# In the first chunk, the high and low parts of a piece are made one unit earlier

## The reference

```
xn  = layernorm(x)
q   = xn @ wq.T                      # 16 heads of 128 (no position) + 64 (rotary)
kv  = xn @ wkv_a.T                   # latent of 128 + one rotary key of 64
kv_cache = rmsnorm(latent) * kv_norm_w
q_lat  = q_nope @ wkv_b[:, :128]     # per head, to the latent width
scores = (q_lat @ kv_cache.T + q_pe @ k_pe.T) * scale, causal
out    = softmax(scores) @ kv_cache @ wkv_b[:, 128:]   # per head
y = x + out @ wo.T + (xn @ ternary(w_ffn).T + b_ffn)
```

## Time and profile before

| | |
|---|---|
| median of 3 runs | 1833.46 us (1831.61 to 1834.55) |
| profiled execution | 1835.66 us, its span 1833.6 us |
| mean granted clock of PE | 0.974 of full speed |
| PE busy | 1715.1 us (94% of the span) |
| DVE, POOL, ACT busy | 1210.3, 1008.5, 848.9 us |
| first chunk, slots 0 to 15 | about 185 to 432 us of the span |

### The profile page before, as it was taken

The page is one execution under the profiler, slowest core; times in us unless marked ns, Lnnn a source line. Parts: engine busy times, 40 slices in busy tenths (PEclk is TensorE's granted clock), DMA queues, the critical chain, the costliest instruction groups (busy, mean ns, idle before and its releaser), DMA issues. The chain is left out here.

```text
span 1833.6 us, 28210 instructions
## 1 busy us (share of the span) xinstructions
PE 1715.1 (94%) x9326; PEld 1448.6 (79%) x9326; DVE 1210.3 (66%) x2801; ACT 848.9 (46%) x1358; POOL 1008.5 (55%) x635
## 2 busy tenths in 40 slices
PE   6998788888999999999999999999999999999996
PEld 5887677666777777778888888888888888888885
DVE  4765465665677667667777767767677666666763
ACT  4554344443444455345544554544544544554442
POOL 4674544443465555455565565565646555565654
PEclk9888899998999999999999999999999999999999
DMA  6995345464766666647555555566756565555553
GB/s 198 372 331 212 105 138 172 134 203 135 196 164 169 173 164 170 195 133 207 151 155 161 144 153 159 158 191 164 191 131 152 146 163 130 158 153 129 148 131 107
DMA packets 127680, 309.12 MB, mean 169 GB/s; under 512 B 29554, under 2 KB 42099, under 8 KB 126388
## 3 DMA queue, kind: packets, MB, share of 16 engines
q1 hardware_dynamic: 98784, 227.04, 44.0%
q10 hardware_dynamic: 28756, 80.35, 16.1%
HBM read 113.28 MB, written 34.60 MB: 81 GB/s over the span
## 5 line engine op out<-in xcount | busy, mean ns | idle before, releaser
L1416 POOL TENSOR_TENSOR pT<-pT,pT_h 128x1024 fp32r<-128x1024 f32 x320 | 688.8, 2181 | 419.8 <-ACT pT_h L1322 418.2
L1196 DVE TENSOR_SCALAR_CACHE_REDUCE probs<-p_score 128x512 f32<-128x512 f32 (+3 forms) x640 | 381.4, 602 | 370.4 <-PE p_score L1124 219.3
L1301 ACT ACTIVATE probs<-probs,neg_max 128x128 f32<-128x128 f32 (+15 forms) x256 | 307.6, 1202 | 438.0 <-DVE neg_max L1202 373.8
L1322 ACT ACTIVATE pT_h<-pT 128x1024 fp32r<-128x1024 f32 x320 | 291.3, 963 | 254.7 <-PE p_out L1144 173.6
L1218 DVE STREAM_TRANSPOSE turned<-probs 128x1024 f32<-128x1024 f32 (+7 forms) x384 | 341.6, 915 | 42.5 <-ACT probs L1301 38.0
L1144 PE MATMUL p_out<-pT_h,V_h 128*128 128x256 f32 (+3 forms) x1024 | 302.7, 296 | 26.6 <-POOL pT L1416 26.5
L1144 PE MATMUL p_out<-pT,V_h 128*128 128x256 f32 (+3 forms) x1024 | 304.2, 297 | 0.0
L1144 PE MATMUL p_out<-pT_h,V_l 128*128 128x256 f32 (+3 forms) x1024 | 303.7, 297 | 0.0
L1124 PE MATMUL p_score<-Kp,qp_h 128*128 128x512 f32 (+3 forms) x640 | 236.3, 369 | 15.3 <-POOL qp_l L1408 15.3
L1124 PE MATMUL p_score<-Kn_h,q_h 128*128 128x512 f32 (+3 forms) x640 | 241.6, 377 | 2.9 <-DVE q_l L1241 2.4
L1144 PEld LDWEIGHTS p_out<-pT_h,V_h 128*128 128x128 f32 x1024 | 196.8, 192 | 51.4 <-issue 34.8
(11 more groups left out here) (135 smaller groups left out, 2352.0 us busy)
## 6 DMA issues: line engine op xcount, KB each, us to landing
pT<-turned SPq DMA_DIRECT2D x384, 128.0 KB, 3.3
Wq<-wq_scr ACTq DMA_DIRECT2D x63, 512.0 KB, 4.7
Wv<-wv_scr SPq DMA_DIRECT2D x63, 512.0 KB, 4.0
pT<-turned SPq DMA_DIRECT2D x192, 112.0 KB, 3.8
pT<-turned SPq DMA_DIRECT2D x192, 96.0 KB, 2.5
pT<-turned ACTq DMA_DIRECT2D x128, 128.0 KB, 3.9
Wp<-wp_scr SPq DMA_DIRECT2D x31, 512.0 KB, 4.7
pT<-turned SPq DMA_DIRECT2D x192, 80.0 KB, 2.8
```

Source lines behind the costliest of these rows:

```text
L1196: dve.tensor_scalar(probs[row % ROW_RING][:, b * CW:b * CW + width], p_score[n % SCORE_RING][:, 0:width], SCALE, LOWEST, ALU.mult, ALU.max ...
L1301: act.activation(probs[row % ROW_RING][:, 0:width], probs[row % ROW_RING][:, 0:width], ACT.Exp, bias=neg_max[p][:, i:i + 1], scale=1.0, ac ...
L1322: act.activation(high.rearrange("p r t i q -> p r t (i q)"), low.bitcast(F32).rearrange("p r t i q -> p r t (i q)"), ACT.Copy).then_inc(p_ ...
L1416: pool.tensor_tensor(low.rearrange("p r t i q -> p r t (i q)"), low.bitcast(F32).rearrange("p r t i q -> p r t (i q)"), high.bitcast(F32). ...
```

## The change

One condition in `high_place`. For the first three groups of a piece whose next slot is in the first chunk (phase 0) the place is now unit 0 of slot s+2, where it was unit 1. Pieces 0 to 14 are concerned; piece 14's place is in slot 16, the first of the second chunk. All their groups have k below 3.

```diff
 def high_place(s, k):
 
     if k < HIGH_RING:
-        return (s + 1, units_of(s + 1) - 1) if phase(s + 1) == 1 else (s + 2, 0 if phase(s + 1) == 3 else 1)
+        return (s + 1, units_of(s + 1) - 1) if phase(s + 1) == 1 else (s + 2, 0 if phase(s + 1) in (0, 3) else 1)
     return s + 2, value_unit(s + 2, k - HIGH_RING)
```

## The result

The changed kernel took 1811.16 us in the median of 4 runs (1810.88 to 1812.61), the kernel before 1834.01 us in 4 runs beside it (1831.61 to 1838.35): ratio 0.9874, 95% interval 0.9855 to 0.9894. The forecast was 1815.3 us, with a range from 1810 to 1828. The gain is 22.9 us where 18.2 were forecast.

The account below looks back on a forecast made before the run. PE, busy 94% of the span, was taken as the bound. Terms 17.0 + 0.6 - 0.7 - 1.1 + 2.4 = 18.2 us gave 1815.3 us; own range 1811 to 1821, with rival 1 1810 to 1828.

Parts of the forecast that it names:

- What started the high groups: In odd slots, ACT's issue of the exchange DMAs, not landing data; start at 322.2 instead of 325.37 us in slot 9.
- POOL's order: In odd slots POOL starts the low groups only after the rotary addition, though the first high part came about a microsecond earlier.
- Odd slots: Slots 3 to 13: POOL wait of 1.49 us goes, plus 1.6 of low clock in five slots; 17.0 us gained.
- Slot 2: The first slot concerned loses its wait of 0.6 us.
- The slack: In odd slots PE could start at about 325.9 us and is ready at 328.31: 2.4 us of slack.
- The new wait for L1408: Even slots: PE waits about 1.45 us for the low rotary query at the fourth score product, covering the `Wv` wait.
- Even slots 4 to 12: 7.3 us of new waits, less 4.6 for `Wv` and 2.0 for POOL: net loss 0.7 us, bounds 0 to 3.
- Slots 14 and 15: ACT comes later to the load of `xT` in slot 14, needed in slot 15: loss 1.1 us, bounds 0 and 2.2.
- Slot 16: Groups start 2.4 us earlier, cutting PE's 2.63 us wait for POOL: gain 2.4 us, bounds 0 and 2.63.
- half of the clock's share not won: Slow end of the forecast's own range, 1821 us: half the gain from avoiding the low clock fails.
- Rival 1: Clock falls behind the new wait in even slots, six times 1.6 us: 1825 us; chance 0.24.
- Rivals 2 and 3: Odd slots: late landing keeps PE's wait, 1832 us, chance 0.10; or blocks ACT's exponential and exchange, 1843.5 us, chance 0.08.

Follow-up runs that it names:

- e1: Kernel before with only ACT's high groups moved to unit 0, POOL's low groups staying in unit 1 behind the rotary addition: 1830.77 us, ratio 0.9961.
- e2: Kernel before with only POOL's low groups moved to unit 0, ACT's high groups staying in unit 1 behind the exchange: 1838.61 us, ratio 1.0011.
- e10: Changed kernel with ACT's high groups in the first chunk behind the first row's exponential, still ahead of the exchange's DMAs: 1812.43 us, ratio 0.9858 to the kernel before.
- a1: The changed kernel run again, unedited: 1818.92 us, ratio 0.9893 to the kernel before.
- a2: The changed kernel run a third time, unedited: 1813.6 us, ratio 0.9873 to the kernel before.
- e4: Kernel before with unit 0 only for piece 14, used in slot 16: 1834.19 us, ratio 0.9982.
- e8: Kernel before with unit 0 only for even pieces 0 to 14, used in even slots 2 to 16: 1826.57 us, ratio 0.9953.
- e6: Changed kernel with SP issuing quarter 2 of the first chunk's exchange right behind quarters 0 and 1, ahead of Wv's load: 1810.79 us, ratio 0.9848 to the kernel before.
- e3: Kernel before with unit 0 only for odd pieces 1 to 13, used in odd slots 3 to 15: 1829.05 us, ratio 0.9962.

## Why the prediction was right, step by step

- *What started the high groups* was the exchange's issue on ACT, not the landing: right for the odd slots. ACT's move alone brings their start from 8.1 to 4.3 us into the slot (e1), with the DMAs ahead they start at 8.1 (e2), and the exponential may stay ahead (e10). The issue was 2.7 us of that delay; another 0.7 was ACT's wait for the piece. In the even slots landing and issue lay close together: the groups, which now wait for the landing, start 4.5 to 5.1 us in, against 5.1 to 5.3 before.
- *POOL's order.* The prediction named the rotary addition as a second obstacle in odd slots but did not price the two moves apart. e1 and e2 do: ratios of 0.9961 and 1.0011.
- *Odd slots*: 1.49 us of wait and 1.6 of clock were forecast, 3.1 together, and 1.49 in slot 3. Measured in slots 5 to 13: 3.27, 3.29, 3.20, 3.12 and 3.08; in slot 3 1.75. Sum 17.7 against 17.0. Slot 2 gave 0.9, not 0.6. That the wait and the clock are two costs is shown inside the kernel before: slot 3 took 16.49 us with the wait alone, slots 5 to 13 took 17.83 to 18.04 with both. The slack was 2.4 us by the forecast, and no odd slot waited for POOL any more.
- *The new wait for L1408*: 1.45 us forecast, 1.47 to 1.49 measured. That it takes the place of the wait for `Wv`: right.
- *Even slots 4 to 12*: a net loss of 0.7 us forecast. Four of them gained 0.07 to 0.16 us each, 0.5 together. Slot 12 lost 1.4 by a fall of the clock. The sum, a loss of 0.9, is near the forecast by luck: the mechanism costs nothing here, the clock did.
- *Slots 14 and 15*: this term was mis-sized. A loss of 1.1 us was forecast, because ACT comes to the load of `xT` later. The issue is indeed later, 8.90 us into slot 14 instead of 8.13. But `p_rot` starts 6.34 us into slot 15, against 6.30 before, so nothing of it reached PE. Instead slot 15 was shorter by 2.5 us (29.13 to 26.63 us, to the first narrow score product of slot 16). I do not count that as the change's: in a1, a2 and e10, whose first chunk is as in this one, the same stretch took 30.05, 25.59 and 25.69 us. The profiles in which ACT has the old order in slot 15 took 29.13 (before), 29.33 (e4), 30.21 (e8) and 27.15 (e2), so a share of the change in it is not excluded either. The `p_rot` there ran at a clock of 0.50 before, 0.65 in this profile, as these windows of the kernel before and of the changed one show.

```profile
415.73:421.20 5.47, 5.47 (x14) 4.33 (x14) 0.00 (x0) 1.57 (x2) 1.68 (x1) 0.50 0.78 182
```

```profile
398.63:403.10 4.47, 4.47 (x14) 3.57 (x15) 0.00 (x0) 1.91 (x4) 0.78 (x1) 0.65 0.78 158
```

- *Slot 16*: 2.4 us forecast, 2.3 measured, with the wait for POOL down from 2.63 to 0.44 us.

Up to slot 17 this is 0.9 + 1.75 + 15.96 - 0.9 + 2.5 + 2.3 = 22.5 us in the two profiled executions, which is 18.2 of the forecast, 3.6 of slots 14 and 15, and small errors. Without the 2.5 us of slot 15 it is 20.0. The spans differ by 26.3 us. Most of the rest lies at the start of the third chunk, where the kernel before ran at a clock of 0.88 and the changed one at 1.00 with the same program:

```profile
744.50:773.30 28.80, 24.67 (x106) 19.65 (x106) 15.58 (x35) 10.20 (x17) 10.89 (x6) 0.88 0.76 219
```

```profile
723.10:748.10 25.00, 22.00 (x105) 17.48 (x105) 15.55 (x35) 10.17 (x17) 10.93 (x6) 1.00 0.92 260
```

In a1 and a2, whose program is the changed one word for word, the same products took 30.50 us at a clock of 0.89 (a1, 726.5 to 757.0) and 24.70 us at 1.00 (a2, 724.6 to 749.3). So this too comes and goes from one execution to the next. It stays open whether the shift by the change alters how often. The three ratios of the changed kernel (0.9873 to 0.9893) stand for 19.6 to 23.3 us. The forecast's 18.2 us is a ratio of 0.9901, which lies inside a1's interval and just outside the other two (0.9894 and 0.9895): the mechanism was right, and the sum somewhat small.

Two readings of the prediction do not come out of its own terms. Its range for the forecast, 1811 to 1821, is said to be the even slots' loss at nothing with the clock of slot 2, and half of the clock's share not won; with its 0.7, 1.6 and half of 8.0 us these give 1813.0 and 1819.3. And it names a new wait in slot 14 that its sum leaves out; slot 14 took 12.76 us against 12.72, so this cost nothing.

- *Rival 1* was given 0.24 as an alternative to the forecast. It came true in part: the clock fell behind one of the six new waits in each of five profiles in which they stand alone (changed, a1, a2, e6, e10), and behind two of six in e3. In slot 12 a fall followed the wait in the changed kernel and a1, and none in a2, e6 and e10. The Trainium skill ("TensorE: Matmul & The Clock Gate", Part 1, "What's actually happening") says that the monitor runs freely and does not start anew with the kernel. These counts fit that; they do not show it. The forecast should have carried it as a term, about 1.6 us for every sixth wait, and not as all or nothing.
- *Rivals 2 and 3* fell: in slots 5 to 13 the landing came 4.2 to 4.7 us into the odd slots, well ahead of the 8.1 at which either would have begun. Only in slot 15, which waits for `xT`, did the groups start 8.9 us in, as before, and PE did not wait for them there.

## What to carry to other kernels

Where an engine both computes and issues DMAs, read what ended just before a late operation, and not only the releaser that the view names: here the high groups started 0.05 to 0.11 us behind the end of the issue in slots 2 to 14 of the kernel before, and the order of the two was what counted in the odd slots. When an order is written out for two engines, move the chain on both, and look at both parities of a slot; one half can cost as much as the other wins. Price a removed PE wait together with the low clock behind it, and look for the chain that does not start earlier when PE does, because the next wait is there and its size can be read off the rows of before.

## What the runs showed of the hardware

- The granted clock fell from 2.4 to 1.2 GHz behind waits of PE of 2 us and less, and in these counts more often the more PE had waited. Waits of 0.63 and 1.48 us, 1.0 us of work apart, stood in 24 odd slots of before, e1, e4 and e8: 20 were 1.3 to 1.6 us longer than the other four (17.83 to 18.05 against 16.46 to 16.49). In slot 9 of the kernel before the first of the two is this one, and the second is in the earlier trace rows:

```profile
327.34 0.73 PE L1156 MATMUL p_result<-Wv,o_h 128*128 128x512 f32 x2 [0.63 <-DVE acc L1259]
```

- Waits of 0.63 and 0.67 to 0.73 us, as far apart, stood in the six odd slots of e2: no fall. A lone wait of 1.48 us stood in 36 even slots of the changed kernel, a1, a2, e6, e10 and e3: the clock fell behind seven. A lone wait of 2.00 us stood in the six even slots of e2: it fell behind five. These waits stand at different places of different slots, so that their length and spacing alone decide is not shown. A fall made the slot 1.3 to 1.7 us longer; in e2's slot 14, where the clock stayed low longer, it took 3.4.
- ACT issued a DMA of the exchange in 0.51 to 1.15 us (median 0.62, 64 DMAs before 440 us in the kernel before), and compute that stood behind four of them waited 2.6 to 2.7 us for them. But issue ran ahead of compute: in the changed kernel's slot 9 the first one went out at 313.50, ahead of the start of the exponential before it in the program (314.14).
- The low groups took 3.60 us on POOL before, when DVE did not rotate beside them, and 3.66 with DVE's rotation beside them, which itself kept its 0.66 and 2.79 us (slot 9 in both).
